# Quaternion memory stage of a four-layer kernel: pairs of components added on VectorE and GpSimd ahead of TensorE's identity products

## The chip, the cores and the metric

The kernel runs on 1 core of a Trainium2 chip. The metric is device time in microseconds, the median of the runs. The core's compute engines, as the rows name them, are PE (TensorE, matrix products into PSUM), DVE (VectorE), ACT (ScalarE) and POOL (GpSimd); SP issues DMAs. SBUF is the working memory of all engines and PSUM the memory that PE writes; POOL reads and writes SBUF alone.

## What is computed

Four layers over 4096 tokens of 128 channels: a time-mixing attention with a scan, a mixture of 8 experts with one chosen, a quaternion memory, and a mixture of 32 experts with four chosen. The change is in the third layer, the memory:

```
keys = (x @ Wk.T + bk).reshape(B, L, N_QUAT, 4)
keys = keys / jnp.maximum(knorm, NORM_EPS)
values = (x @ Wv.T + bv).reshape(B, L, N_QUAT, 4)
bound = quat_mul(values, keys)
memory = jnp.cumsum(bound, axis=1)
retrieved = quat_mul(memory, quat_conj(keys)).reshape(B, L, D)
retrieved = retrieved / jnp.sqrt(positions)[None, :, None]
normed = (retrieved - mu) / jnp.sqrt(var + LN_EPS) * ln_g + ln_b
return x + (normed @ Wo.T + bo)
```

A quaternion product has four terms for each of its four components. `retrieved`, the second product, is what the change is about.

## The kernel before

The memory stage takes the tokens in 8 tiles of 512 (TILES = 8), each in four subtiles of 128 tokens (SUB = 4, index `s`). Tokens lie on the 128 partitions, so a subtile has 128 channels on the free axis, and the four terms of a quaternion product (QC = 4, index `m`) make a tile of 512 elements per partition. Each engine has a program of its own, written out in order: `weave` walks 16 steps per tile, and in each step an engine runs what its functions `tail` (the tile before), `main` (this tile), `ahead` and `norm` (the next ones) hold for that step. Semaphores alone tie the engines together. From the last two tiles on, steps of the last layer (`look`, `route`) are woven in.

The second quaternion product of a tile runs like this.

- DVE forms `early_n` (which lies in PSUM, in the bank named `c_v`) and `memory_n` (SBUF), the normed memory of subtiles 0, 1 and of 2, 3 (step 8 and 9, L2018 and L2023).
- Step 10: DVE multiplies key and `early_n` for subtiles 0 and 1 into `read[:, s]` (L2029, in the rows `c_read<-c_key,c_v`), and POOL key and `memory_n` for subtiles 2 and 3 (L2337, `c_read<-c_key,c_memory_n`). Each product writes all four terms.
- Steps 12 to 15, one subtile each: PE adds the four terms up in the PSUM bank `bank_r` (`c_r`) by four products with the identity matrix (L1842). Between the first and the second subtile stand PE's transposes of a later tile's input (L1797), and after the last the key projection of the next tile (L1801, L1803, `c_k`).
- Meanwhile DVE and POOL form `real` (L2034 and L2342), POOL then goes on to `bound` of the next tile (L2331, `c_bound`), and in tiles 1 to 6 DVE makes in steps 11 and 15 a slice each of the low parts of the last layer's weights (`make_lo`, L1995, `d_lo<-state_and_wide,d_hi`, both operands in SBUF). In tile 1 it also makes four small constants (L2002 to L2006).
- DVE subtracts in `tail` step 0 of the next tile: `got` = 2 `real` - `bank_r` (L2043), after `real_pool` and `read_out`. Behind it stand in DVE's program `bound` of the next tile (L2012), the moments, the norm of the keys and so on, up to the next `memory_n`.

In tile 7 DVE's routing of the last layer's first tile stands in between: behind step 10's products it forms the routing weights (L2133 to L2139, `d_weight`), PE transposes them between the second and the third subtile's identity products (L1896), ACT copies them, and SP sends them through `pair_weights` in HBM back to SBUF, spread over the partitions, where DVE's `c_bound<-c_v,state_and_wide` (L2160) waits for them.

Of the kernel before, what the change touches and what calls it, by code (L numbers as in the profile page):

```python
# [9 lines left out]
ALU = mybir.AluOpType  # L10
# [125 lines left out]
def need(engine, semaphore, value):  # L136

    if not isinstance(value, int) or value > 0:
        engine.wait_ge(semaphore, value)
# [1298 lines left out]
QUATS, QC = P // 4, 4  # L1438
# [80 lines left out]
def memory_and_top4(nc, block, x_tok, consts, weights, spare, loaded, out_dram, moe, results, row_stored):  # L1519
# [3 lines left out]
    with ExitStack() as ctx:  # L1523
        def sb(name, shape, dt=F32):
            return ctx.enter_context(nc.sbuf_tensor("c_" + name, shape, dt))
# [4 lines left out]
        def sem(name):  # L1530
            return nc.alloc_semaphore("c_" + name)

        def w(name):
            return weights[:, CW_AT[name][0]:CW_AT[name][1]]
# [22 lines left out]
        read = sb("read", [P, SUB, QC, P])  # L1557
# [32 lines left out]
        read_dve, read_pool = sem("read_dve"), sem("read_pool")  # L1590
# [19 lines left out]
        def spread_component(ap):  # L1610

            return ap.rearrange("p (q m) -> p m q", m=QC).unsqueeze(3).broadcast_to([P, QC, QUATS, QC])
# [13 lines left out]
        def dw(name):  # L1626
            return moe["small"][:, DW_AT[name][0]:DW_AT[name][1]]
# [52 lines left out]
        ROUTING = 14  # L1680
        BY_TANH = (4, 5)
        NORMED_AT = 10

        def split_cols(c):

            n, part = divmod(c, SPLITS)
            width = UNITS * P // SPLITS
            return n, slice(part * width, (part + 1) * width)

        def weave(engine, norm, ahead, main, tail, look, route, unit, end):  # L1690
# [29 lines left out]
            for step in range(STEPS):  # L1720
                norm(0, 0, step)
            for step in range(NORMED_AT):
                norm(1, 1, step)
            for step in range(STEPS):
                ahead(0, 0, step)
                if step >= NORMED_AT:
                    norm(1, 1, step)
# [63 lines left out]
        def _(pe):  # L1791
# [24 lines left out]
            def main(i, h, step):  # L1816
                if step in (1, 3, 5, 7):
                    s = step // 2
                    if s < 2:
                        pe.wait_ge(bound_dve, 2 * i + s + 1)  # L1820
                    else:
                        pe.wait_ge(bound_pool, 2 * i + s - 1)
                    need(pe, memory_ready, SUB * i + s - 1)
                    carried = h or s
                    for m in range(QC):
                        mm = pe.matmul(bank_m[s % 2][:, 0:P], w("upto"), bound[:, s, m, :],  # L1826
                                       start=(m == 0), stop=(m == QC - 1 and not carried))
                    if carried:
                        pe.wait_ge(memory_ready, SUB * i + s)
                        before = memory[:, h, s - 1, :] if s else memory[:, 1 - h, SUB - 1, :]  # L1830
                        mm = pe.matmul(bank_m[s % 2][:, 0:P], w("last"), before, start=False, stop=True)
                    mm.then_inc(memory_out, 1)
                if step >= 12:
                    s = step - 12
                    if s == 0:
                        need(pe, got_ready, i)
                    if s < 2:
                        pe.wait_ge(read_dve, 2 * i + s + 1)
                    else:
                        pe.wait_ge(read_pool, 2 * i + s - 1)  # L1840
                    for m in range(QC):
                        mm = pe.matmul(bank_r[:, s * P:(s + 1) * P], ident, read[:, s, m, :],  # L1842
                                       start=(m == 0), stop=(m == QC - 1))
                    if s == SUB - 1:
                        mm.then_inc(read_out, 1)

# [105 lines left out]
        def _(dve):  # L1952
# [45 lines left out]
            def main(i, h, step):  # L1998
                if step in (11, 15) and 0 < i <= 3 * SPLITS // 2:
                    make_lo(2 * i - 2 if step == 11 else 2 * i - 1)  # L2000
                if step == 14 and i == 1:
                    dve.memset(mask_b[:, SUB, :], 0.0)  # L2002
                    dve.tensor_copy(strict[:, :], dw("strict"))
                    dve.tensor_copy(ones_b[:, :], dw("ones"))
                    dve.wait_ge(wg_made, 1)
                    dve.tensor_tensor(wg_lo[:, :], dw("wg"), wg_hi[:, :].bitcast(F32), ALU.subtract).then_inc(small_made, 1)  # L2006
                if step == 0:
                    dve.wait_ge(valuen_ready, 2 * (i + 1))
                    dve.wait_ge(key_ready, i + 1)
                    need(dve, memory_out, SUB * i)  # L2010
                    for s in (0, 1):
                        dve.tensor_tensor(in_quats(bound[:, s, :, :]), in_quats(key[:, h, s, :, :]),  # L2012
                                          spread_component(early_value[:, s, :]), ALU.mult).then_inc(bound_dve, 1)
                if step == 8:
                    dve.wait_ge(memory_ready, SUB * (i + 1) - 2)
                    dve.wait_ge(valuen_ready, min(2 * i + 3, 2 * TILES) if isinstance(i, int) else 2 * i + 3)
                    need(dve, real_ready, i)
                    dve.tensor_tensor(by_quat(early_n), by_quat(memory[:, h, 0:2, :]), per_quat(rnorm[:, h, 0:2 * QUATS]),  # L2018
                                      ALU.mult).then_inc(memoryn_ready, 1)
                if step == 9:  # L2020
                    dve.wait_ge(memory_ready, SUB * (i + 1))
                    need(dve, real_pool, i)
                    dve.tensor_tensor(by_quat(memory_n[:, :, :]), by_quat(memory[:, h, 2:4, :]), per_quat(rnorm[:, h, 2 * QUATS:]),  # L2023
                                      ALU.mult).then_inc(memoryn_ready, 1)
                if step == 10:
                    dve.wait_ge(memoryn_ready, 2 * (i + 1))
                    need(dve, read_out, i)
                    for s in (0, 1):
                        dve.tensor_tensor(in_quats(read[:, s, :, :]), in_quats(key[:, h, s, :, :]),  # L2029
                                          spread_component(early_n[:, s, :]), ALU.mult).then_inc(read_dve, 1)  # L2030
                if step == 12:
                    need(dve, got_ready, i)
                    k0 = key[:, h, 0:2, 0, 0:P:QC]
                    dve.tensor_tensor(components(real[:, 0:2, :]), components(early_n),  # L2034
                                      k0.unsqueeze(3).broadcast_to([P, 2, QUATS, QC]), ALU.mult).then_inc(real_ready, 1)
# [268 lines left out]
        def _(pool):  # L2304
# [15 lines left out]
            def main(i, h, step):  # L2320
                if step == 4:
                    pool.wait_ge(xn_ready, i + 1)
                    need(pool, x_ready, i - 1)
                    pool.tensor_tensor(kept[:, h, :, :], xn[:, h, :, :], x_tok[:, bass.ds(SUB * i, SUB), :],
                                       ALU.add).then_inc(kept_ready, 1)
                if step == 0:
                    pool.wait_ge(valuen_ready, 2 * i + 1)
                    pool.wait_ge(key_ready, i + 1)
                    need(pool, memory_out, SUB * i)
                    for s in (2, 3):  # L2330
                        pool.tensor_tensor(in_quats(bound[:, s, :, :]), in_quats(key[:, h, s, :, :]),  # L2331
                                           spread_component(value_n[:, s - 2, :]), ALU.mult).then_inc(bound_pool, 1)
                if step == 10:
                    pool.wait_ge(memoryn_ready, 2 * (i + 1))
                    need(pool, read_out, i)
                    for s in (2, 3):
                        pool.tensor_tensor(in_quats(read[:, s, :, :]), in_quats(key[:, h, s, :, :]),  # L2337
                                           spread_component(memory_n[:, s - 2, :]), ALU.mult).then_inc(read_pool, 1)
                    need(pool, got_ready, i)
                    for s in (2, 3):  # L2340
                        k0 = key[:, h, s, 0, 0:P:QC]
                        r = pool.tensor_tensor(real[:, s, :].rearrange("p (q c) -> p q c", c=QC),  # L2342
                                               memory_n[:, s - 2, :].rearrange("p (q c) -> p q c", c=QC),
                                               k0.unsqueeze(2).broadcast_to([P, QUATS, QC]), ALU.mult)
                    r.then_inc(real_pool, 1)
# [165 lines left out]
```

## Time and profile before

| | |
|---|---|
| median of 3 runs | 820.4 us (819.52 to 821.27) |
| the profiled execution's own time | 819.28 us |
| its span, first to last instruction | 817.3 us |
| PE busy | 727.6 us, 89% of the span |
| DVE busy | 602.2 us, 74% |
| POOL busy | 490.0 us, 60% |
| ACT busy | 485.6 us, 59% |
| identity products of the change (L1842) | 256 passes, 31.2 us busy, started from 373.2 to 482.0 us |

A busy share is an average over stages with different limits: the memory stage, from about 342 to 483 us, is a sixth of the span, and the last layer's, from 483 us on, is bounded by its own products. What an edit in the memory stage is worth has to be read from that stage's own order of waits. In the rows an fp32 product with the identity shows as two passes, so that four products are "x8".

### The profile page before, as it was taken

The page shows a single profiled execution, that of the slowest core. Times are in us where ns is not written, and L with a number is a line of the kernel's source. Part 1 is how long each engine was busy: PE and PEld are TensorE (multiplying, and loading weights), DVE is VectorE, ACT ScalarE, POOL GpSimd, SP SyncE. Part 2 cuts the span into 40 slices and gives each one's busy share as a digit, 9 for nine tenths or more (in the row PEclk, how much of TensorE's full clock was granted, in tenths as well). Part 3 has the DMA queues.
Part 4 walks back from the last instruction along what each step waited for, and adds up shares of the span by engine and source line. Part 5 has one row for each costly group of instructions (what it writes and reads, how often), then busy time and mean ns, then how long its engine had stood idle before and what let it go on. Part 6 is the DMA issues. An engine that isn't in the chain of part 4 may idle for free.

```text
span 817.3 us, 14378 instructions
## 1 busy us (share of the span) xinstructions
PE 727.6 (89%) x4027; PEld 549.6 (67%) x4028; DVE 602.2 (74%) x1377; ACT 485.6 (59%) x1045; POOL 490.0 (60%) x498
## 2 busy tenths in 40 slices
PE   4599999999868799668999979999999999999996
PEld 2345554555447689657888867777778787878784
DVE  3489999999965445347888758786868686868673
ACT  3567778664435367446566556666666665666553
POOL 3577668788753544436878745555555555555564
PEclk9889999999979999859999998999999999999999
DMA  8700000000011355210000036363636364646450
GB/s 246 244 0 1 0 1 14 8 8 14 14 40 44 107 137 142 67 41 28 14 1 1 2 74 137 74 149 79 145 83 140 84 140 89 134 93 132 100 122 13
DMA packets 38265, 60.47 MB, mean 74 GB/s; under 512 B 3776, under 2 KB 17728, under 8 KB 37808
## 3 DMA queue, kind: packets, MB, share of 16 engines
q1 hardware_dynamic: 35920, 54.93, 28.5%
q0 software_dynamic: 2272, 4.67, 1.7%
q8 instruction: 32, 0.52, 0.3%
q14 instruction: 41, 0.34, 0.1%
HBM read 51.31 MB, written 8.28 MB: 73 GB/s over the span
## 4 chain that ended last, share of the span: by engine, by line
PE 66%; DVE 17%; issue 7%; ACT 4%; POOL 2%; DMA 2%; DVEq 1%; another core or an unknown queue 0%; ACTq 0%; POOLq 0%; SPq 0%
DVE state_and_wide L803 4%; PE a_vb L635 4%; PE c_m L1861 4%; PE c_m L1826 4%; PE c_m L1863 3%; PE c_m L1862 3%; PE c_r L1842 3%; PE a_front L481 3%; PE a_vb L644 2%; PE a_y L644 2%; DVE a_vb L787 2%; PE c_v L1861 2%; PE c_r L1911 2%; PE c_r L1910 2%; PE c_r L1913 2%
## 5 line engine op out<-in xcount | busy, mean ns | idle before, releaser
L2379 POOL TENSOR_TENSOR d_hid_lo<-c_bound,d_hid_hi 128x512 fp32r<-128x512 f32 x136 | 175.6, 1292 | 141.3 <-ACT d_hid_hi L2289 139.9
L2289 ACT ACTIVATE d_hid_hi<-c_bound 128x512 fp32r<-128x512 f32 x136 | 85.1, 626 | 38.0 <-DVE c_bound L2160 36.8
L1367 POOL TENSOR_TENSOR ducts_and_memory_weights<-a_r,state_and_wide 128x512 f32<-128x512 f32 x64 | 75.0, 1181 | 25.2 <-DVE state_and_wide L803 19.8
L803 DVE TENSOR_TENSOR_SCAN state_and_wide<-a_decay,state_and_wide,a_vb 128x512 f32<-128x512 f32 x64 | 81.0, 1268 | 0.1
L2151 DVE TENSOR_TENSOR c_m<-c_bound,c_m 128x512 f32<-128x512 f32 x64 | 44.3, 691 | 23.5 <-PE c_m L1863 17.5
L2151 DVE TENSOR_TENSOR c_v<-c_bound,c_v 128x512 f32<-128x512 f32 x64 | 44.3, 692 | 22.0 <-PE c_v L1863 16.3
L1861 PE MATMUL c_m<-d_x_hi,d_hi 128*128 128x512 f32 x136 | 56.3, 414 | 3.6 <-DVE c_bound L2160 3.3
L2279 ACT ACTIVATE c_bound<-c_m 128x512 f32<-128x512 f32 x60 | 35.7, 595 | 33.7 <-PE c_m L1863 33.1
L2279 ACT ACTIVATE c_bound<-c_k 128x512 f32<-128x512 f32 x60 | 35.7, 595 | 33.4 <-PE c_k L1863 32.9
L1863 PE MATMUL c_m<-d_x_hi,d_lo 128*128 128x512 f32 x136 | 54.4, 400 | 0.0
L1862 PE MATMUL c_m<-d_x_lo,d_hi 128*128 128x512 f32 x136 | 54.0, 397 | 0.0
L787 DVE TENSOR_TENSOR a_vb<-a_k,a_vb 128x512 f32<-128x512 f32 x64 | 43.3, 688 | 8.1 <-PE a_vb L535 7.9
L973 DVE TENSOR_TENSOR a_lerp<-a_vb,b_b 128x512 f32<-128x512 f32 x39 | 27.0, 691 | 28.2 <-PE a_vb L635 20.0
L1350 POOL TENSOR_TENSOR a_xf<-a_lerp,a_xt 128x512 f32<-128x512 f32 x32 | 34.7, 1093 | 18.2 <-DVE a_lerp L780 18.1
L635 PE MATMUL a_vb<-a_td_hidden,a_m 128*128 128x128 f32 x312 | 42.5, 281 | 3.4 <-DVE a_lerp L973 1.8
L1376 POOL DMA_INDIRECT rows_in<-a_rows,a_index x32 | 31.9, 996 | 21.3 <-DVE a_index L953 15.2
L2160 DVE TENSOR_TENSOR c_bound<-c_v,state_and_wide 128x512 f32<-128x512 f32 x56 | 38.7, 691 | 7.0 <-DMA state_and_wide<-pair_weights 4.0
L481 PE MATMUL a_front<-a_m,a_weights 128*128 128x512 f32 x64 | 35.2, 644 | 8.5 <-ACT a_m L1149 8.4
L635 PEld LDWEIGHTS a_vb<-a_td_hidden,a_m 128*128 128x128 f32 x312 | 38.9, 197 | 4.4 <-issue 2.9
L2160 DVE TENSOR_TENSOR c_bound<-c_m,state_and_wide 128x512 f32<-128x512 f32 x56 | 38.7, 691 | 2.5 <-POOL d_hid_lo L2379 0.7
L534 PE MATMUL a_vb<-a_v_hi,a_spread 128*128 128x512 f32 x64 | 38.7, 605 | 0.6 <-issue 0.5
L1252 ACT ACTIVATE a_xf<-a_lerp 128x512 f32<-128x512 f32 x39 | 24.5, 629 | 22.8 <-DVE a_lerp L973 8.3
(376 smaller groups left out, 2151.1 us busy)
## 6 DMA issues: line engine op xcount, KB each, us to landing
state_and_wide<-pair_weights SPq DMA_DIRECT2D x64, 512.0 KB, 11.5
b_w<-in_w SPq DMA_DIRECT2D x2, 2048.0 KB, 12.1
state_and_wide<-in_moe SPq DMA_DIRECT2D x16, 204.0 KB
a_xf<-rows_in SPq DMA_DIRECT2D x39, 64.5 KB
state_and_wide<-results SPq DMA_DIRECT2D x8, 256.0 KB, 2.7
out<-c_read SPq DMA_DIRECT2D x8, 256.0 KB, 2.3
a_weights<-in_mixing SPq DMA_DIRECT2D x1, 1077.0 KB, 7.1
shape_consts<-in_consts SPq DMA_DIRECT2D x1, 744.0 KB, 4.4
```

Source lines behind the costliest of these rows:

```text
L481: mm = pe.matmul(front[n % 3][:, :], w("mix2")[:, f * P:(f + 1) * P], m1[:, 0, :], start=True, stop=True)
L635: mm = pe.matmul(bank_h[h][:, f * P:(f + 1) * P], w1_now[:, h, f * P:(f + 1) * P], xin_t[:, h, :], start=True, stop=True)
L803: dve.tensor_tensor_scan(state[:, j, seq_cols(h, 1)], decay[:, h, :], vb[j % 3][:, :], first, ALU.mult, ALU.add).then_inc(scan_ready, 1)
L1367: pool.tensor_tensor(rs[:, j, :], rr[:, h, :], state[:, j, seq_cols(h, 0)], ALU.mult).then_inc(rs_ready, 1)
L1861: pe.matmul(out, weights_hi, moving_hi, start=start, stop=False)
L1862: pe.matmul(out, weights_hi, moving_lo, start=False, stop=False)
L1863: return pe.matmul(out, weights_lo, moving_hi, start=False, stop=stop)
L2151: dve.tensor_tensor(bank_3[r][:, :], silu[:, r, :], bank_3[r][:, :], ALU.mult).then_inc(product_ready, 1)
L2160: dve.tensor_tensor(hidden[:, r, :], bank_3[r][:, :], w_wide[:, u - 1, :], ALU.mult).then_inc(hidden_ready, 1)
L2279: act.activation(silu[:, r, :], bank_1[r][:, :], ACT.Silu).then_inc(silu_ready, 1)
L2289: act.activation(hid_hi[:, n % HALVES, :], hidden[:, r, :], ACT.Copy).then_inc(hi_ready, 1)
L2379: pool.tensor_tensor(hid_lo[:, n % HALVES, :], hidden[:, r, :], hid_hi[:, n % HALVES, :].bitcast(F32), ALU.subtract).then_inc(lo_ready, 1)
```

## The change

PE makes two identity products per subtile in place of four. The terms 2 and 3 are first added to the terms 0 and 1 in place: one addition on DVE for subtiles 0 and 1, one on POOL for subtiles 2 and 3, each of 2 x 256 = 512 elements per partition, with both operands and the result in `read` in SBUF. Each addition waits for its own engine's two products by a semaphore, and PE waits for the addition instead of the product.

```
+        PAIRED = 3
...
                     if s == 0:
                         need(pe, got_ready, i)
-                    if s < 2:
-                        pe.wait_ge(read_dve, 2 * i + s + 1)
-                    else:
-                        pe.wait_ge(read_pool, 2 * i + s - 1)
-                    for m in range(QC):
+                    pe.wait_ge(read_dve if s < 2 else read_pool, PAIRED * (i + 1))
+                    for m in range(2):
                         mm = pe.matmul(bank_r[:, s * P:(s + 1) * P], ident, read[:, s, m, :],
-                                       start=(m == 0), stop=(m == QC - 1))
+                                       start=(m == 0), stop=(m == 1))
...
                     for s in (0, 1):
                         dve.tensor_tensor(in_quats(read[:, s, :, :]), in_quats(key[:, h, s, :, :]),
                                           spread_component(early_n[:, s, :]), ALU.mult).then_inc(read_dve, 1)
+                    dve.wait_ge(read_dve, PAIRED * i + 2)
+                    dve.tensor_tensor(read[:, 0:2, 0:2, :], read[:, 0:2, 0:2, :], read[:, 0:2, 2:QC, :], ALU.add).then_inc(read_dve, 1)
...
                     for s in (2, 3):
                         pool.tensor_tensor(in_quats(read[:, s, :, :]), in_quats(key[:, h, s, :, :]),
                                            spread_component(memory_n[:, s - 2, :]), ALU.mult).then_inc(read_pool, 1)
+                    pool.wait_ge(read_pool, PAIRED * i + 2)
+                    pool.tensor_tensor(read[:, 2:, 0:2, :], read[:, 2:, 0:2, :], read[:, 2:, 2:QC, :], ALU.add).then_inc(read_pool, 1)
```

DVE's program from the second product of a middle tile (tile 4) on, before:

```order
L2029 TENSOR_TENSOR c_read<-c_key,c_v 128x512 x2
L1995 TENSOR_TENSOR d_lo<-state_and_wide,d_hi 128x544
L2034 TENSOR_TENSOR c_real<-c_v,c_key 128x256
L2059 TENSOR_TENSOR x_tok<-c_o,c_kept 128x512
L1995 TENSOR_TENSOR d_lo<-state_and_wide,d_hi 128x544
L2043 SCALAR_TENSOR_TENSOR c_got<-c_real,c_r 128x512
L2012 TENSOR_TENSOR c_bound<-c_key,c_v 128x512 x2
```

and with the change, where the lines of the source have moved by two:

```order
L2027 TENSOR_TENSOR c_read<-c_key,c_v 128x512 x2
L2030 TENSOR_TENSOR c_read<-c_read 128x2x256
L1993 TENSOR_TENSOR d_lo<-state_and_wide,d_hi 128x544
L2034 TENSOR_TENSOR c_real<-c_v,c_key 128x256
L2059 TENSOR_TENSOR x_tok<-c_o,c_kept 128x512
L1993 TENSOR_TENSOR d_lo<-state_and_wide,d_hi 128x544
L2043 SCALAR_TENSOR_TENSOR c_got<-c_real,c_r 128x512
L2010 TENSOR_TENSOR c_bound<-c_key,c_v 128x512 x2
```

The addition now stands ahead of the first slice of low parts; nothing else on DVE has moved. POOL's program at the same place, with the change:

```order
L2337 TENSOR_TENSOR c_read<-c_key,c_memory_n 128x512 x2
L2340 TENSOR_TENSOR c_read<-c_read 128x2x256
L2344 TENSOR_TENSOR c_real<-c_memory_n,c_key 128x128 x2
L2331 TENSOR_TENSOR c_bound<-c_key,c_value_n 128x512 x2
L2352 TENSOR_TENSOR c_var_eps<-c_moments,products_and_memory_weights 128x4
```

Before, the same rows stand there without the addition. PE has in tile 7, before, these rows:

```order
L1842 MATMUL c_r<-c_read,ident 128x128 x8
L1896 MATMUL c_d<-ident,d_weight 32x128 x4
L1842 MATMUL c_r<-c_read,ident 128x128 x8
L1861 MATMUL c_k<-d_x_hi,d_hi 128x512
```

With the change each of the two groups of identity products there is half as long, and the order is the same.

## Rows read from the trace of the kernel before

**Rows 1.** The page, busy time by engine: us, share of span, instructions

```profile
PE 727.6 (89%) x4027; PEld 549.6 (67%) x4028; DVE 602.2 (74%) x1377; ACT 485.6 (59%) x1045; POOL 490.0 (60%) x498
```

**Rows 2.** Chain that ended last, tile 4: start us, us, what

```profile
432.62 0.89 PE c_r L1842 x8
...
433.95 2.68 PE c_r L1842 x24
436.63 0.43 PE c_k L1801
...
438.17 0.94 PE c_m L1826 x6
```

**Rows 3.** Timeline of tile 4: start us, us, engine, line, what [idle before <-releaser]

```profile
431.20 1.28 DVE L2029 TENSOR_TENSOR c_read<-c_key,c_v 128x512 f32<-128x512 f32 x2
431.24 3.01 POOL L2337 TENSOR_TENSOR c_read<-c_key,c_memory_n 128x512 f32<-128x512 f32 x2 [0.36 <-DVE c_memory_n L2023]
...
434.22 1.35 POOL L2342 TENSOR_TENSOR c_real<-c_memory_n,c_key 128x128 f32<-128x128 f32 x2
...
435.53 2.50 POOL L2331 TENSOR_TENSOR c_bound<-c_key,c_value_n 128x512 f32<-128x512 f32 x2
...
436.83 0.69 DVE L2043 SCALAR_TENSOR_TENSOR c_got<-c_real,c_r 128x512 f32<-128x512 f32 x1 [2.00 <-PE c_r L1842]
```

**Rows 4.** Timeline in narrow windows, single instructions of tile 4

```profile
432.40 0.72 DVE L1995 TENSOR_TENSOR d_lo<-state_and_wide,d_hi 128x544 fp32r<-128x544 f32 x1
...
432.47 1.78 POOL L2337 TENSOR_TENSOR c_read<-c_key,c_memory_n 128x512 f32<-128x512 f32 x1
...
433.97 0.87 DVE L1995 TENSOR_TENSOR d_lo<-state_and_wide,d_hi 128x544 fp32r<-128x544 f32 x1
...
434.22 0.94 POOL L2342 TENSOR_TENSOR c_real<-c_memory_n,c_key 128x128 f32<-128x128 f32 x1
```

**Rows 5.** The same, in tile 1

```profile
389.46 0.35 DVE L2003 CAST d_strict<-ducts_and_memory_weights 128x128 bf16<-128x128 f32 x1
...
389.69 0.46 POOL L2342 TENSOR_TENSOR c_real<-c_memory_n,c_key 128x128 f32<-128x128 f32 x1
389.73 0.49 DVE L2004 CAST d_ones<-ducts_and_memory_weights 128x128 bf16<-128x128 f32 x1
...
390.52 1.27 POOL L2331 TENSOR_TENSOR c_bound<-c_key,c_value_n 128x512 f32<-128x512 f32 x1
390.53 1.84 DVE L1995 TENSOR_TENSOR d_lo<-state_and_wide,d_hi 128x544 fp32r<-128x544 f32 x1
```

**Rows 6.** Windows, `got` to next products, then to `got`: us, busy by engine, clock

```profile
436.83:445.90 9.07, 8.22 (x62) 7.08 (x61) 8.75 (x28) 6.39 (x19) 5.79 (x10) 1.00 0.01 3
445.90:451.77 5.87, 5.81 (x46) 5.34 (x46) 3.64 (x7) 3.24 (x8) 5.83 (x6) 1.00 0.00 0
```

**Rows 7.** Groups by line: busy us, mean ns of one | idle before

```profile
L1957 DVE TENSOR_TENSOR x_tok<-x_tok,state_and_wide 128x512 f32<-128x512 f32 x8 | 5.4, 680 | 6.3 <-DMA state_and_wide<-results 6.3
L2324 POOL TENSOR_TENSOR c_kept<-c_xn,x_tok 128x512 f32<-128x512 f32 x8 | 10.2, 1271 | 0.0
L1350 POOL TENSOR_TENSOR a_xf<-a_lerp,a_xt 128x512 f32<-128x512 f32 x32 | 34.7, 1093 | 18.2 <-DVE a_lerp L780 18.1
```

**Rows 8.** Chain that ended last, tile 7 and after

```profile
477.21 0.70 DVE c_read L2029
...
478.04 2.02 PE c_r L1842 x16
480.06 0.45 PE c_d L1896 x4
...
483.60 6.67 DMA state_and_wide<-pair_weights
...
490.36 0.70 DVE c_bound L2160
```

**Rows 9.** Windows, the start of the last layer

```profile
483.00:500.00 17.00, 13.52 (x53) 10.99 (x53) 9.74 (x29) 8.14 (x17) 6.68 (x8) 0.80 0.95 211
```

## The prediction

> **What bounds the kernel now.** I read the busy times first. PE is busy 89% of the span [rows 1], and the change takes work from PE, which speaks for a gain. So the second view is the chain that ended last, inside the memory stage. In tile 4 it runs through the identity products, 0.89 us for the first subtile and 2.68 us for the other three, with no wait between them but PE's own transposes, then through the key projection to the products of `bound` at 438.17 [rows 2]. In tile 4 PE is what ends last.
>
> The third view is the timeline of the same stretch, and there the slack is thin. I count from DVE's first product at 431.20. DVE's `got` starts at 5.63, released by PE after 2.00 us of idle time; POOL meanwhile makes its two products (3.01 us) and `real` (1.35 us), which ends at 4.37, and then `bound` [rows 3]. Both DVE's idle 2.00 us and POOL's lead of 1.26 us (5.63 - 4.37) are short beside an instruction of 512 elements. From `got` to the next tile's first product pass 9.07 us, of which DVE is busy 8.75 [rows 6]: that stretch is DVE's, and a later `got` moves everything behind it. So each microsecond by which `got` comes later costs the tile a microsecond, and a `got` that came earlier would gain one.
>
> The fourth view is the same timeline cut so narrow that single instructions show. POOL's second product takes 1.78 us where a POOL instruction of this size takes 1.27, and it does so while DVE runs the slice of `d_lo`, whose operands both lie in SBUF: that slice runs from 432.40 to 433.12, and POOL's ends at 434.25, 1.13 us after [rows 4, 5]. In tile 1 it is the other way round: POOL's `bound` starts at 390.52, DVE's slice at 390.53, and the slice ends at 392.37, 1.84 us long and 0.58 after POOL's end (391.79) [rows 5]. The two engines take turns, an instruction at a time. DVE's products of key and `early_n` do not meet this: their second operand lies in PSUM, and beside them POOL's first product (3.01 - 1.78 = 1.23 to the start of the second) is not stretched [rows 3, 4].
>
> Who goes first? In both directions it is the one that came first: POOL by 0.01 us at 390.52; DVE's second slice, waiting since 433.97, ahead of POOL's `real` of 434.22, which is stretched to 0.94 us [rows 4, 5]. Two DVE instructions in a row don't keep the place: the cast at 389.46 waited for POOL and ran to 389.81, the next cast came at 389.73, but POOL's `real`, which had come at 389.69, went first, undelayed at 0.46 us, and the cast took 0.49 [rows 5].
>
> The Trainium skill states this as a rule (SBUF — State Buffer, section "Who interferes with whom"): a DVE instruction with two SBUF inputs and a GpSimd instruction that reads SBUF exclude each other for their whole length, and issue order decides who blocks. The trace agrees (1.84 us where DVE's slice takes 0.72). It speaks against this change, since both new additions are of that kind; without the rule, as a sum of bare durations, the change would come out near 820.5 us, with it as below.
>
> **The change, part by part.** Removed: half of PE's identity products, half of 0.89 + 2.68 = 3.57 us, so 1.79 us a tile and 14.3 us over eight tiles if PE stayed last [rows 2]. Added: an addition on DVE (an in-SBUF addition of 512 elements takes 0.68 us) and one on POOL (1.27 us by `c_kept` of this stage, 1.09 by the lowest row of that size) [rows 7]. No row shows an addition of this shape in place; I take 0.68 and 1.27, since nearest in stage and size, and keep 1.09 for the range. I follow one tile with two slices (tile 4), in us after DVE's first product.
>
> - POOL's second product is next in POOL's queue when its first ends, at 1.27 (432.47). DVE's addition waits for DVE's second product, which ends at 1.28, and so comes at about 1.32, some 0.04 later. POOL came first, ends at 1.27 + 1.27 = 2.54, and DVE's addition ends 0.55 after it (0.58 for 544 elements, less 32) at **3.09**. PE's first identity product, which started at 1.42 [rows 2], starts at 3.14.
> - POOL's addition comes at 2.6, waits for DVE's, and ends 1.13 after it, at **4.22**. DVE's first slice comes at 3.0, so later, and ends at 4.22 + 0.58 = 4.80.
> - PE: two products 0.45 to 3.59, transposes 0.44 to 4.03, two products to 4.48, four more to 5.37. PE is now early.
> - POOL's `real` waits for the slice: 0.32 to the first's end (434.22 + 0.94 - 434.84) and 0.41 for the second, **5.53**; `bound` follows at 5.50 and holds until 6.77.
> - DVE's second slice comes 0.85 after the first's end (433.12 to 433.97), at 5.65: 0.15 behind POOL's `bound`. It waits until 6.77 and ends at **7.35**.
> - `got`, next in DVE's queue, starts at 7.3, against 5.63 in tile 4 and 5.87 in tile 5 [rows 6]: **+1.65 and +1.45**, in the mean 1.55.
>
> So the stall goes from "DVE waits for PE" to "DVE's slice waits for POOL's `bound`", and what is late next is `bound`, the moments and the normed memory, all of DVE's 9.07 us.
>
> The tiles. Tiles 2 to 6 have two slices: 5 x 1.55 = 7.75. Tile 1 has four constants between, two casts and a subtraction from SBUF among them; by the same turns the second cast falls behind POOL's second `bound` (6.85 + 1.13 = 7.98), the slice ends at 8.7 and `got` starts about 8.65: +2.8. Tile 0 has no slice; PE starts at 3.14 in place of 0.7 but has 1.79 less to do: +0.5 (PE starts today as soon as DVE's first product is done, in tile 7 0.83 after its start [rows 8]; 3.14 - 0.83 - 1.79 = 0.52). Tile 7 has none either, but PE's transposes of the routing weights stand behind four identity products, and DVE's `d_weight` behind the addition. They started 2.85 after DVE's product (480.06 - 477.21) [rows 8]; now 3.14 + 0.89 = 4.03: **+1.2**, and this is on the path, through the load of 6.67 us for which DVE's `c_bound` at 490.36 waits [rows 8].
>
> Sum: 0.5 + 2.8 + 7.75 + 1.2 = 12.25 us, on the profiled execution's own 819.3: 831.5. The median lies 1.1 above that execution, so 832.6. With POOL's addition at 1.09 each of tiles 1 to 6 is 0.18 shorter, 1.1 in all. I take 832. After 490 nothing is changed, and the last layer moves as a whole.
>
> **The rivals.**
> - *DVE's addition goes first* (0.20). The two come within 0.05 us, and a place that is given away by turns, or POOL's request a little after its start, would turn it. Then the addition ends at 1.85, POOL's second product at 2.98, the slice at 3.56, POOL's addition at 4.69; the second slice, coming at 4.41, is ahead of `real`, `real` ends at 6.0 and `got` starts at 6.05: +0.3 in the mean of tiles 2 to 6, 1.5 in all, tile 1 +1.5, tiles 0 and 7 together +0.5: 3.5 us, 824. Beside it (0.05), DVE's first slice follows the addition without giving way: `got` at 6.2, also 824.
> - *The additions don't meet* (0.08). Were DVE's addition unlike the slices, it would end at 2.0, and only the slices would hold POOL: `real` ends at about 5.6, `got` starts at 5.65 where it did, and the saving of PE is eaten by POOL's 1.27: 820.5, no change.
> - *Faster* (0.05). PE's saving arrives where POOL's addition ends before PE's first four identity products do. With nothing held up it would end at 2.54 + 0.08 + 1.09 = 3.71, `real` at 4.6, `got` at 4.65: 1.0 to 1.2 a tile, up to 8.5 in all, 812. It is decided by POOL's second product: it must take 1.27 and the slices must find gaps. Against it: that product takes 1.78 today [rows 4].
> - *PE's clock falls as well* (0.07). PE's busy time falls to 8.22 + 5.81 - 1.79 = 12.2 us [rows 6] in a tile of 9.07 + 7.3 = 16.4, with two idle stretches of about 1.7 (up to DVE's addition, and from the key projection to `bound`). Today the clock stays at 1.00, which is 2.4 GHz, in the tiles [rows 6], and 17 us with PE's wait for the load in them show 0.80 [rows 9], that is 6.8 us at the lower level, 1.2 GHz. One such stretch more costs up to 3.4 us: 836; one in every tile would go beyond 850.
>
> **How the numbers follow.** The forecast has 0.55; its own range is 829 to 835. The two cases near 824 hold 0.25, no change 0.08, faster 0.05, the clock 0.07. The range 822.5 to 836.5 takes in the forecast, those at 824 and a single clock stretch. A difference under 0.2% (1.6 us) can't be told from none. Slower by more: 0.55 + 0.25 + 0.07 = 0.87, less 0.01 of the cases near 824 that end within it: 0.86; same 0.08 + 0.01 = 0.09; faster 0.05.
>
> **What would show it.** In the timeline of a middle tile: DVE's addition at about 1.8 us in place of 0.68, POOL's second product back at 1.27 where it took 1.78, POOL's addition near 1.6, DVE's first slice near 1.8, the second near 1.7, and `got` without idle time before it, released by nothing of PE. PE's wait for DVE's addition, about 1.7 us a tile, new in the waits. The distance from one `got` to the next 9.07 + 7.3 = 16.4 in place of 14.7 and 14.9. Wrong would be: POOL's second product still stretched (DVE went first), or `got` still waiting for PE (POOL's addition is then dearer than I have it, or PE's clock has fallen).

## The result and the profile after

The changed kernel takes 839.46 us (median of 4 runs, 837.64 to 843.2), the one before 820.12 (with a fourth run beside the three of the first table): ratio 1.0237, 95% interval 1.021 to 1.0264. It is slower by 19.3 us. The prediction said 832 with a range up to 836.5, so the sign was right and the time lies 3 us outside the range.

The page of the changed kernel, busy time by engine, answers to [rows 1]:

```profile
PE 729.7 (87%) x3899; PEld 549.3 (66%) x3900; DVE 627.4 (75%) x1385; ACT 485.7 (58%) x1045; POOL 501.8 (60%) x506
```

PE has 128 passes fewer and yet is busy 2.1 us longer, and DVE is busy 25.2 us longer for eight added instructions of 0.68. Both are signs of instructions that last longer than they need: DVE's because they wait for POOL, PE's because its clock is lower.

The timeline of tile 4 answers to [rows 3, 4]: start us, us, engine, line, what, and the idle time ahead of it with its releaser.

```profile
442.66 1.28 DVE L2027 TENSOR_TENSOR c_read<-c_key,c_v 128x512 f32<-128x512 f32 x2
442.70 2.50 POOL L2337 TENSOR_TENSOR c_read<-c_key,c_memory_n 128x512 f32<-128x512 f32 x2 [0.35 <-DVE c_memory_n L2021]
443.98 1.77 DVE L2030 TENSOR_TENSOR c_read<-c_read 128x512 f32<-128x512 f32 x1
...
445.28 1.60 POOL L2340 TENSOR_TENSOR c_read<-c_read 128x512 f32<-128x512 f32 x1
445.67 1.79 DVE L1993 TENSOR_TENSOR d_lo<-state_and_wide,d_hi 128x544 fp32r<-128x544 f32 x1
...
445.90 0.68 PE L1840 MATMUL c_r<-c_read,ident 128*128 128x128 f32 x4 [1.83 <-DVE c_read L2030]
...
448.16 2.98 POOL L2331 TENSOR_TENSOR c_bound<-c_key,c_value_n 128x512 f32<-128x512 f32 x2
...
448.32 1.69 DVE L1993 TENSOR_TENSOR d_lo<-state_and_wide,d_hi 128x544 fp32r<-128x544 f32 x1
449.93 0.67 DVE L2043 SCALAR_TENSOR_TENSOR c_got<-c_real,c_r 128x512 f32<-128x512 f32 x1
```

Counted from DVE's first product at 442.66: DVE's addition comes at 1.32 and ends at 3.09 (predicted 1.32 and 3.09), POOL's two products take 2.50 together, where they took 3.01, and end at 2.54 (2.54), POOL's addition ends at 4.22 (4.22), the first slice at 4.80 (4.80), POOL's `bound` starts at 5.50 (5.50), the second slice comes at 5.66 and ends at 7.35 (7.35), and `got` starts at 7.27 (7.3). No idle time stands ahead of `got`. PE waits 1.83 us for DVE's addition, and its first identity product comes at 3.24 (predicted 3.14).

The windows of the changed kernel (from `got` to the next tile's first product, or from there to `got`) answer to [rows 6, 9]; the third number from the end is the granted clock:

```profile
389.63:398.37 8.74, 5.56 (x38) 4.60 (x38) 8.70 (x11) 4.63 (x10) 7.87 (x7) 1.00 0.01 3
398.37:409.62 11.25, 9.41 (x51) 8.32 (x51) 8.86 (x28) 4.84 (x16) 4.42 (x9) 0.70 0.08 23
442.66:449.93 7.27, 5.38 (x38) 4.42 (x38) 7.24 (x7) 3.08 (x8) 7.15 (x7) 1.00 0.01 2
449.93:459.00 9.07, 6.91 (x53) 6.11 (x53) 8.75 (x29) 6.38 (x19) 5.81 (x10) 1.00 0.00 1
482.06:495.21 13.15, 11.20 (x67) 9.94 (x66) 9.33 (x41) 6.86 (x18) 5.63 (x10) 0.76 0.00 1
495.21:503.25 8.04, 5.71 (x29) 5.22 (x28) 4.57 (x8) 1.85 (x4) 4.92 (x5) 0.50 0.03 8
```

The kernel before, behind `got` of tile 1 and of tile 6:

```profile
392.51:401.58 9.07, 8.16 (x61) 7.02 (x60) 8.75 (x28) 6.62 (x19) 5.59 (x10) 1.00 0.10 29
466.02:477.21 11.19, 8.88 (x73) 7.80 (x70) 9.33 (x41) 6.75 (x18) 5.46 (x10) 1.00 0.00 1
```

In tile 4 the clock is at 1.00 (2.4 GHz) and the stretch behind `got` has its old 9.07 us. Behind tile 1's `got` the clock is at 0.70 and the stretch takes 11.25 in place of 9.07, with DVE hardly busier than before (8.86 against 8.75); PE's busy time is what has grown, from 8.16 to 9.41 us. So it is behind tile 6's (13.15 in place of 11.19), and in tile 7 PE runs at 0.50, which is 1.2 GHz. There the weights for the last layer leave late, and the last wait of the memory stage (the load for DVE's `c_bound`) ends at 511.05. From the chain that ended last, in tile 7 and after:

```profile
495.21 1.29 DVE c_read L2027 x2
...
498.44 2.05 PE c_r L1840 x8
500.49 0.87 PE c_d L1894 x4
...
501.99 1.65 DMA pair_weights<-d_w_turned
...
504.44 6.52 DMA state_and_wide<-pair_weights
...
511.05 0.70 DVE c_bound L2160
```

The four transposes of the weights take 0.87 us where they took 0.45 [rows 8]. They start 5.28 us after DVE's product (predicted 4.03, before 2.85), and the DMA of the weights starts 6.78 after it (3.94 before).

The account, from the first product of tile 0 to that `c_bound`: 117.91 us before (372.45 to 490.36), 137.24 after (373.81 to 511.05), a difference of 19.33 us. The spans of the two profiled executions differ by 19.5 us (836.8 against 817.3), so nearly the whole cost lies here.

| term | predicted | measured |
|---|---|---|
| tile 0, product to `got` | +0.5 | +1.50 |
| tile 1 | +2.8 | +2.89 |
| tiles 2 to 6 | +7.75 | +7.98 (1.70, 1.69, 1.64, 1.41, 1.54) |
| tile 7, product to the load's end | +1.2 | +2.69 |
| between `got` and the next product, all tiles | 0 | +4.27 (0.11 behind tile 0, 2.18 behind tile 1, 1.96 behind tile 6) |
| sum | 12.25 | 19.33 |

### The profile page after: what moved, and what is told of

It reads as the page before. It is cut to its first block and busy times, and to the rows that moved or that the text cites. A ratio compares the mean times of both kernels' runs of the same rounds, so it can differ in the third digit from the quotient of the medians.

```text
span 836.8 us, 14138 instructions
## 1 busy us (share of the span) xinstructions
PE 729.7 (87%) x3899; PEld 549.3 (66%) x3900; DVE 627.4 (75%) x1385; ACT 485.7 (58%) x1045; POOL 501.8 (60%) x506
## 5 line engine op out<-in xcount | busy, mean ns | idle before, releaser
L1367 POOL TENSOR_TENSOR ducts_and_memory_weights<-a_r,state_and_wide 128x512 f32<-128x512 f32 x64 | 75.0, 1182 | 25.2 <-DVE state_and_wide L803 19.8
L635 PE MATMUL a_vb<-a_td_hidden,a_m 128*128 128x128 f32 x312 | 44.7, 291 | 1.1 <-ACT a_td_hidden L1247 0.9
L1827 PE MATMUL c_m<-c_bound,ducts_and_memory_weights 128*128 128x128 f32 x256 | 37.4, 296 | 6.4 <-DVE c_bound L2010 6.4
L635 PEld LDWEIGHTS a_vb<-a_td_hidden,a_m 128*128 128x128 f32 x312 | 41.1, 206 | 2.1 <-issue 1.0
```

Of the source, the lines that this page charges most:

```text
L635: mm = pe.matmul(bank_h[h][:, f * P:(f + 1) * P], w1_now[:, h, f * P:(f + 1) * P], xin_t[:, h, :], start=True, stop=True)
L1367: pool.tensor_tensor(rs[:, j, :], rr[:, h, :], state[:, j, seq_cols(h, 0)], ALU.mult).then_inc(rs_ready, 1)
```

## The experiments

All times in us after DVE's first product of a tile, unless they are of the whole kernel.

**DVE's addition alone.** POOL's addition is left out, and PE takes four products of subtiles 2 and 3.

```
-                    pool.tensor_tensor(read[:, 2:, 0:2, :], read[:, 2:, 0:2, :], read[:, 2:, 2:QC, :], ALU.add).then_inc(read_pool, 1)
...
+                    terms = 2 if s < 2 else QC
+                    for m in range(terms):
```

> DVE's addition alone; subtiles 2 and 3 keep four identity products each. Theory (the two engines take turns at SBUF, the first to come goes first): in a middle tile, counted from DVE's first product, DVE's addition ends at 3.1 as with the whole change, POOL's `real` slips in behind it, and PE, which starts at 3.14 and has 0.45 + 0.44 + 0.45 + 1.79 of work, ends at 6.27: `got` starts at 6.4, released by PE. Over the tiles +3.3, tile 1 about +1, tile 0 +1.25, the routing weights +1.2: 827 us, clock mostly at 1.00. Rival (an addition costs what it takes, 0.68): PE starts at 2.0 and `got` at 5.2: 816 to 820 us.

Measured: 837.88 us, ratio 1.0209 (1.0153 to 1.0265), against 820.77 for the kernel before. The turns were as expected, DVE's addition ended at 3.09, and `got` started at 6.80 in the undisturbed tiles (PE started 0.1 later than reckoned, and `got` follows PE's last pass by 0.2). By an estimate, 0.4 us more than expected in each of tiles 2 to 5 and 0.7 more in tile 1, that would be some 829. But tile 3 took 9.70, and tiles 0 and 7 took 8.30 and 8.42. Windows of tile 3 and tile 4, from product to `got`:

```profile
423.30:433.00 9.70, 8.04 (x38) 7.38 (x38) 6.08 (x7) 3.23 (x8) 7.20 (x6) 0.65 0.00 1
442.07:448.87 6.80, 4.98 (x38) 4.36 (x38) 6.09 (x7) 3.06 (x7) 6.75 (x6) 1.00 0.00 0
```

The same 38 passes on PE, at a clock of 0.65 and of 1.00: 2.9 us lie between. The rival (816 to 820) is out. The expected 827 was missed by 11 us, and the clock was not in that sum; how much of the miss is the clock's, the same kernel with PE kept busy shows below.

**POOL's addition alone.** The other half: DVE's addition is left out, subtiles 0 and 1 keep four products.

> POOL's addition alone; subtiles 0 and 1 keep four identity products. Theory of turns: DVE's first slice still comes ahead of POOL's second product, which stays at 1.78 us, DVE's second slice goes ahead of POOL's addition, which ends at 4.76; PE's last four products end at 5.7 and `got` starts at 5.84, near where it does without the change: 821 us within 1.5, POOL's addition about 1.6 us long, no stretch at the lower clock in the tiles. Rival (POOL is the engine that can't afford it, whatever DVE does): half or more of the change's 19 us, 829 or above.

Measured: 825.16 us, ratio 1.0049 (1.0024 to 1.0074). Single instructions of a middle tile (DVE's first product at 435.34):

```profile
436.63 1.77 POOL L2339 TENSOR_TENSOR c_read<-c_key,c_memory_n 128x512 f32<-128x512 f32 x1
438.11 0.87 DVE L1997 TENSOR_TENSOR d_lo<-state_and_wide,d_hi 128x544 fp32r<-128x544 f32 x1
438.48 1.63 POOL L2342 TENSOR_TENSOR c_read<-c_read 128x512 f32<-128x512 f32 x1
...
440.16 1.16 PE L1844 MATMUL c_r<-c_read,ident 128*128 128x128 f32 x8 [1.19 <-POOL c_read L2342]
```

The addition ended at 4.77 (expected 4.76), but `got` started at 6.18, 0.34 later than reckoned: PE's start and `got`'s wait take 0.1 and 0.2 more than I had. The time lies 2.7 us above the expected 819.5 to 822.5, of which five tiles of 0.34 make 1.7. In tile 7, against what was expected, the clock was at 0.74 up to `got`, and the DMA of the weights started 4.89 us after DVE's product in place of 3.94: 0.95 more. The rival's 829 is out. POOL's addition by itself is the cheap half.

**The whole change, PE kept busy.** The clock was the open point. Seven identity products of no use, whose result is overwritten, stand ahead of each of PE's two new waits (the fillers, from here on; they show as fourteen passes).

```
                     if s == 0:
                         need(pe, got_ready, i)
+                        for _ in range(FILL):
+                            pe.matmul(bank_r[:, 0:P], ident, ident, start=True, stop=True)
...
+                    if s == 0 and i > 0:
+                        need(pe, memory_ready, SUB * i - 1)
+                        for _ in range(FILL):
+                            pe.matmul(bank_m[0][:, 0:P], ident, ident, start=True, stop=True)
```

> The whole change, and seven identity products of no use (ident by ident, overwritten after) ahead of each of PE's two new waits: before the first sum of a tile and before the first product of `bound`. Theory (the change costs 12 us by turns and the rest by PE's clock, which falls where PE idles): the clock stays at 1.00 from tile 1 to tile 6, the distance of `got` is 16.35 us in tiles 2 to 6 and 18 or less from tile 1 to 2, and the time is 831 to 834. Rival (the lower clock costs nothing, since PE waits anyway): 839, as with the change. Third: the fillers themselves are in the way: above 841.

Measured: 834.0 us, ratio 1.0184 (1.013 to 1.0237). Windows behind `got` of tile 1, tile 4 from product to `got`, behind `got` of tile 6, and tile 7:

```profile
398.55:407.62 9.07, 6.94 (x53) 6.07 (x52) 8.75 (x29) 5.55 (x17) 4.60 (x9) 1.00 0.10 29
440.31:447.59 7.28, 7.10 (x55) 6.30 (x56) 7.25 (x8) 3.14 (x8) 7.16 (x7) 1.00 0.01 2
479.72:490.91 11.19, 8.82 (x73) 7.80 (x71) 9.34 (x41) 6.15 (x17) 5.58 (x10) 1.00 0.00 0
490.91:496.76 5.85, 4.48 (x40) 4.20 (x38) 4.59 (x9) 1.06 (x3) 4.93 (x5) 1.00 0.00 0
```

With more work on PE the median is 5.5 us lower, and the slowest of these four runs (837.24) is below the fastest of the changed kernel's four (837.64). All four show a mean granted clock of 0.959 to 0.965, as the kernel before does (0.957 to 0.968); the four of the changed kernel show 0.942 to 0.945. In the profiled executions the stretch from tile 0's first product to the load's end is 3.5 us shorter (133.76 against 137.24). From tile 1 to the load the clock is at 1.00, and 11.25, 13.15 and 8.04 us have become 9.07, 11.19 and 5.85; tile 4's 7.28 is unchanged, since it was never the clock's. Tile 0 still ran partly at the lower clock (`got` at 6.68), and behind it the fillers cost 1.6 us. In tile 7 the chain reads:

```profile
494.06 1.16 PE c_r L1847 x8
495.22 0.45 PE c_d L1901 x4
...
496.31 1.65 DMA pair_weights<-d_w_turned
...
498.76 7.31 DMA state_and_wide<-pair_weights
```

The DMA of the weights starts 5.40 us after DVE's first product (490.91), 1.38 sooner than without the fillers. The load itself took 7.31 us here and 6.52 there, which hides 0.79 of it.

**DVE's addition alone, PE kept busy.** The same test for the first experiment, with the first of the two fillers.

> DVE's addition alone, which took 837.9 where turns account for about 830, with seven identity products of no use on PE ahead of its wait. Theory (the rest is PE's clock, which fell in tiles 0, 3 and 7): no stretch at the lower clock in tiles 1 to 6, `got` at 6.8 after DVE's first product in tiles 2 to 5, also in tile 3 where it was 9.70, and 829 to 832. Rival (the single late tiles are scatter of another kind, not PE's clock): 836 or above.

Measured: 829.27 us, ratio 1.0104 (1.0087 to 1.0121), against 820.5; `got` at 6.75 in tiles 2 to 5. Tile 3, window from product to `got`:

```profile
421.75:428.50 6.75, 6.67 (x52) 6.09 (x52) 6.10 (x7) 3.25 (x8) 6.70 (x6) 1.00 0.02 4
```

It had been 9.70. The mean granted clock of these runs is 0.961 to 0.966, and 0.946 to 0.953 without the filler. About half of what DVE's addition alone cost, 8.6 of 17.1 us, was PE's clock.

**The whole change, both slices together.** DVE's second slice right behind the first.

```
-                if step in (11, 15) and 0 < i <= 3 * SPLITS // 2:
-                    make_lo(2 * i - 2 if step == 11 else 2 * i - 1)
+                if step == 11 and 0 < i <= 3 * SPLITS // 2:
+                    make_lo(2 * i - 2)
+                    make_lo(2 * i - 1)
```

> The whole change with DVE's second slice of low parts right behind the first, in place of ahead of `got`. Theory of turns: it asks before POOL's `bound` and no longer waits for it; in a middle tile the first slice ends at 4.80, the second at 5.7, and `got` starts at 6.5 in place of 7.3: 0.8 us a tile less in tiles 2 to 6, more in tile 1, so 834 to 835 where the change has 839.5. Rival (the place of a slice does not matter, only DVE's sum of work does): `got` at 7.3 and 839.

Measured: 834.11 us, ratio 1.0164 (1.0113 to 1.0214); `got` at 6.56 in tiles 4 to 6 (tiles 2 and 3 had stretches of the lower clock: 7.38, 7.54). So the stall of DVE's slice moves with the place of a slice that is not part of the change. The median is within the expected 834 to 835, but not for the reason given alone: in the profiled execution tiles 4 to 6 gain 0.72 each and tiles 2 and 3 nothing, while the stretch behind tile 6's `got`, in which the clock did not fall this time, is back at 11.18.

**Both together.** The fillers, and the second slice right behind the first.

> The whole change, with the fillers on PE and DVE's second slice right behind the first. If the two costs add (turns and clock), it is 0.7 us a tile below the filled one in tiles 2 to 6: `got` at 6.56 after DVE's first product, 830 to 831. If they share a cause, it stays at 834.

Measured: 833.86 us, ratio 1.0164 (1.0148 to 1.018). The expected 830 to 831 was missed. `got` came at 6.57 as expected, but the stretch behind it took 9.19 to 9.40 in place of 9.07, because the second filler, sized for a longer wait, now ran past its end. The stretch from the first product of tile 0 to the load's end was 129.5 us against 133.8 in the filled kernel; the medians, of 5 and 4 runs on different chips, don't show these 4 us, which the profiled runs lose before the stage (x_tok's first sum at 351.4 against 349.3) and after it.

This run settles tile 0, whose programs are the same in both, since DVE makes no slices there. Windows of tile 0, from product to `got`, here and in the filled kernel:

```profile
374.69:380.45 5.76, 3.37 (x28) 3.04 (x27) 3.38 (x4) 2.59 (x7) 5.64 (x6) 1.00 0.01 1
372.40:379.08 6.68, 4.30 (x28) 3.88 (x27) 3.38 (x4) 3.14 (x8) 6.56 (x7) 0.84 0.00 1
```

The same 28 passes, with the clock at 1.00 and at 0.84: 0.92 us lie between.

**The addition from PSUM.** A version built on this, for tiles 0 to 6. A bank that the memory stage doesn't use before tile 7 takes the products 2 and 3 of subtiles 0 and 1, so that DVE's addition reads only one operand from SBUF; POOL adds nothing; PE takes POOL's first subtile ahead; both of DVE's slices stand right behind the addition.

```
+        ORDER = (2, 0, 1, 3)
...
+                    s = ORDER[step - 12] if i < LAST else step - 12
...
+                        later = bank_d[:, :].rearrange("p (s m c) -> p s m c", s=2, m=2)
+                        for s in (0, 1):
+                            for half, to in ((0, read[:, s, 0:2, :]), (2, later[:, s, :, :])):
+                                dve.tensor_tensor(in_quats(to), in_quats(key[:, h, s, half:half + 2, :]),
+                                                  spread_component(early_n[:, s, :])[:, half:half + 2, :, :],
+                                                  ALU.mult).then_inc(read_dve, 1)
+                        dve.wait_ge(read_dve, PER_READ * i + 4)
+                        dve.tensor_tensor(read[:, 0:2, 0:2, :], read[:, 0:2, 0:2, :], later, ALU.add).then_inc(read_dve, 1)
```

> A version built on what the first runs showed. In tiles 0 to 6 DVE alone adds in pairs, with terms 2 and 3 of subtiles 0 and 1 written to a PSUM bank that is free then, so that its addition has one operand in SBUF; POOL adds nothing; PE takes subtile 2 first, then 0, 1, 3; both slices of low parts stand right behind the addition. Theory of turns: DVE's addition takes 0.7 us and ends at 2.1 after DVE's first product, POOL's second product is back at 1.27, PE has 28 passes without a wait between, and `got` starts at 4.9 in place of 5.6 and 5.9: 5 to 6 us less in all, 814 to 816, the clock at 1.00 in the tiles. Rival (an addition from PSUM waits for POOL as well, or PE's order brings nothing): `got` at 5.6 or later, 820 or above.

Measured: 818.72 us, ratio 0.9979 (0.9963 to 0.9995). The expected 814 to 816 was missed by some 3 us. `got` starts at 5.03 in tiles 2 to 5 (expected 4.9), but at 6.92 in tile 1. Tile 1's timeline says why (DVE's first product at 388.32):

```profile
392.63 2.49 POOL L2348 TENSOR_TENSOR c_bound<-c_key,c_value_n 128x512 f32<-128x512 f32 x2
393.24 0.76 DVE L2010 CAST d_strict<-ducts_and_memory_weights 128x128 bf16<-128x128 f32 x1
...
393.91 1.30 DVE L2011 CAST d_ones<-ducts_and_memory_weights 128x128 bf16<-128x128 f32 x1
```

Each of two small casts waited out one of POOL's `bound`.

**Control: the kernel before with the slices together.**

> Control: the kernel before with DVE's second slice right behind the first, nothing else. PE ends last in these tiles, so `got` stays at 5.6 and 5.9 and the time within 1.5 us of the kernel before. If the slices' place mattered by itself, it would be below 819.

Measured: 822.86 us, ratio 1.0021 (1.0001 to 1.0041). The middle tiles kept 5.6 and 5.9; tile 1 took 6.93 in place of 5.85 for the same two casts. The median is 2.4 us above the kernel before, where 1.5 at most was expected. In the profiled execution tile 7 took 6.85 us up to `got` in place of 5.28, with the clock at 0.75. The seven runs with a mean granted clock of 0.958 took 822.1 to 825.9 us, the five with 0.960 to 0.964 took 817.7 to 821.0. So the slices' place brings no gain by itself, and the clock can fall in tile 7 of a kernel that has no addition at all.

**The addition from PSUM, subtiles in the old order.**

> The version with the addition from PSUM, but PE takes the subtiles as before, 0, 1, 2, 3. PE then starts when the addition is done, at 2.2 in place of 1.3 after DVE's first product, and has 28 passes of 0.11 from there, so `got` starts at 5.7: the saving on PE is eaten by its later start, 819 to 822. If the order of the subtiles does not matter, it is where the reordered version is.

Measured: 830.03 us, ratio 1.0124 (1.0109 to 1.0139). The expected 819 to 822 was missed by 8 us. The undisturbed tiles took 5.85 (expected 5.7). Tile 0 took 8.51 (its window and that of tile 5):

```profile
373.77:382.28 8.51, 6.30 (x29) 6.16 (x29) 2.44 (x6) 2.99 (x8) 5.78 (x6) 0.60 0.00 1
453.76:459.61 5.85, 5.14 (x38) 4.53 (x38) 4.92 (x9) 3.25 (x8) 5.80 (x6) 1.00 0.00 0
```

PE now waits for the addition at the start of each tile, and the clock falls again, in tiles 0, 4 and 7. The order of the subtiles is worth 11 us here (830.03 - 818.72): tiles 2, 3 and 5, at a clock of 1.00, lose 0.8 us each by the wait, tile 0 loses 3.6 and tile 4 2.5, at 0.60 and 0.77.

**The same with tile 1's constants moved.** The reordered version, the memset and the casts in tile 0.

> The version with DVE's addition from PSUM and PE's subtiles reordered, and the four constants of tile 1 moved ahead (memset and the two casts into tile 0, where DVE makes no slices, the small subtraction to the start of tile 1). Theory of turns: in tile 1 `got` started 6.92 after DVE's first product because the casts and the subtraction each waited for a turn behind POOL; without them it starts at 5.0 to 5.1, so 1.7 us less than the version before it: 817, and 3 to 4 us below the kernel before. If tile 1 was late for another reason, its `got` stays at 6.9.

Measured: 816.42 us, ratio 0.9953 (0.9936 to 0.9969), against 820.5: 4 us faster than the kernel before. Single instructions of a middle tile (first product at 430.28), and windows of tile 2:

```profile
431.56 1.28 POOL L2355 TENSOR_TENSOR c_read<-c_key,c_memory_n 128x512 f32<-128x512 f32 x1
431.74 0.69 DVE L2044 TENSOR_TENSOR c_read<-c_read,c_d 128x512 f32<-128x512 f32 x1
432.35 1.07 DVE L2001 TENSOR_TENSOR d_lo<-state_and_wide,d_hi 128x544 fp32r<-128x544 f32 x1
```

```profile
402.06:407.09 5.03, 4.99 (x38) 4.36 (x38) 4.93 (x10) 3.06 (x7) 4.98 (x5) 1.00 0.00 0
407.09:416.20 9.11, 8.21 (x62) 7.08 (x61) 8.79 (x27) 6.45 (x19) 6.42 (x11) 1.00 0.01 3
```

The addition takes 0.69 us beside POOL's product and neither is stretched, while the slice, with both operands in SBUF, waits again. PE has no wait in the first window, and `got` is 0.6 to 0.85 us a tile ahead of [rows 6]; tile 1's started at 5.02. Tile 0's came at 6.47, with the clock at 0.74, where the version before had 4.88 at 1.00; without that, by an estimate from the two, it would be 1.6 us faster still.

## Why the prediction was right and wrong

- **PE ends last before the change, by little.** Right: taking its work away without giving it a wait (the last version) gains 0.6 to 0.85 us in each of tiles 1 to 6.
- **The two engines take turns, the first to come goes first.** Right, to 0.03 us for each step of DVE and POOL in tile 4; PE's first product was 0.10 later than reckoned, which costs nothing where `got` doesn't wait for PE. The case in which DVE's addition goes first was a matter of 0.03 to 0.05 us, and POOL went first in all eight tiles: its second product takes 1.26 again. That the order came out as forecast by so little is in part luck; the prediction gave the other order 0.20. The rule of the Trainium skill (SBUF — State Buffer, "Who interferes with whom") holds here also in its exception: a DVE instruction with one SBUF input does not contend with POOL. The trace agrees: the addition with one operand in PSUM takes 0.69 us beside POOL's product.
- **The terms for tile 1 and tiles 2 to 6** (10.55 us) measured 10.87. Right.
- **"Between `got` and the next tile's first product pass 9.07 us ... that stretch is DVE's."** This is the step that failed, and with it the 0 at which the sum puts these stretches. They are DVE's only while PE runs at 2.4 GHz. Of the 9.07 us PE was busy 8.22 before; where the clock falls, PE becomes the last, and the stretch grows by 2.18 us behind tile 1 and 1.96 behind tile 6. The fillers brought both to nothing.
- **The clock.** The prediction had it as a rival with a chance of 0.07 and a price of 3.4 us for one stretch, with the two idle stretches of 1.7 a tile that bring it about. It came in tiles 0, 2, 3, 6 and 7 and behind tiles 0, 1 and 6. The sum lacks 19.33 - 12.25 = 7.1 us, and the clock is nearly all of it. Measured against the same stretches in the two kernels with fillers, it costs 0.89 in tile 0 (6.66 against 5.77), 2.18 behind tile 1, 0.06 and 0.27 in tiles 2 and 3, 1.96 behind tile 6 and 1.38 in tile 7 up to the DMA of the weights. Together that is 6.7 us. To these come 0.11 behind tile 0, at a clock of 0.93, which no run took apart.
- **What is left.** Tile 0's term of +0.5 is +0.6 at the full clock. Tile 7's +1.2 is +1.46 there (5.40 against 3.94 up to the DMA of the weights): the transposes start at 4.31 in the filled kernel, against the reckoned 4.03. These and smaller differences the other way make up the remaining 0.2 us.
- **"PE is now early"** was read as a reserve. PE early is PE idle, and this is what the clock answered to.
- **The rivals.** "The additions don't meet" and "faster" are out by the timeline. The sum of bare durations would have said 820.5.
- **The price of the lower clock.** The clock fell six times, and each fall cost less than the 3.4 us that the rival has for one: in tiles 2 and 3 next to nothing, since there DVE's slice, and not PE, had been what ends last. How often it would fall, nothing in the rows before foretold.

Why the clock fell where it did, and not in tiles 4 and 5, whose waits are as long (1.83 and 1.39 us in tile 4), stays open. Two of the falls come with a longer idle stretch of PE: 3.94 us ahead of tile 0's first identity product, 2.86 ahead of the first product of `bound` behind tile 1. For the others no idle stretch was longer than in tile 4: 1.29 in tile 2, 1.60 in tile 3, and none above 1.6 from tile 5 up to tile 7's first product. Nor does the length of the wait in tile 0 decide it: PE idled 2.38 and 2.39 us there in the two kernels with both fillers, and 2.23 and 2.17 in the two with the reordered addition from PSUM, and in each pair the clock fell in one and not in the other.

## What to carry to other kernels

Before work is moved from PE to DVE or POOL, look at where the operands lie: here a DVE addition with both operands in SBUF took 1.77 us beside POOL's product in place of 0.68, one with an operand in PSUM 0.69. Then ask how long PE waits after the change, not only whether it ends last: a PE that is relieved and then waits (here 1.3 to 1.8 us in a middle tile) can lose its clock, and the same products then take longer where they do matter (0.87 us in place of 0.45 for four transposes). If it must wait, let it start with what is ready first; the order of four subtiles was worth 11 us, part of it by the clock.

## What was not expected of the hardware

- The granted clock fell with no long idle stretch of PE: behind tile 1 it was at 0.70 after a tile in which PE was busy 5.56 of 8.74 us, with idle stretches of 1.28 and 2.86 us, and in tile 6 it fell with none above 1.6. In the kernel before, with no idle stretch above 1.6 us from tile 0 on, it stayed at 1.00 through all eight tiles.
- Seven useless products (fourteen passes) ahead of each of two waits took 5.5 us off the median, and a tile's same 38 passes, with the clock at 0.65, took 9.70 us in place of 6.80.
- The order in which the second product of POOL and DVE's addition run is decided by 0.03 to 0.05 us and was the same in each of the eight tiles.
